# Negated softmax scale folded into the query weights of a decoder layer's attention

## The reference

```python
q = _mxfp4_matmul(x, wq_codes, wq_scales) + bq      # w = codes * repeat(scales, 32, axis=0)
k = _mxfp4_matmul(x, wk_codes, wk_scales) + bk
v = _mxfp4_matmul(x, wv_codes, wv_scales) + bv
...                                                  # 16 heads of 128
scores = jnp.einsum('bqhd,bkhd->bhqk', q, k) / jnp.sqrt(jnp.float32(HEAD_DIM))
attn = jax.nn.softmax(scores, axis=-1)
out = jnp.einsum('bhqk,bkhd->bqhd', attn, v).reshape(B, S, NUM_HEADS * HEAD_DIM)
return _mxfp4_matmul(out, wo_codes, wo_scales) + bo
```

## Time and profile before

| | before |
|---|---|
| median of 3 runs | 530.16 us (528.49 to 530.91) |
| span of the profiled execution | 527.9 us |
| PE busy | 489.7 us, 93% |
| DVE busy | 405.2 us, 77% |
| ACT busy | 283.8 us, 54% |
| POOL busy | 191.0 us, 36% |

### The profile page before, as it was taken

One profiled execution on the slowest core, in us unless ns is written; L12 is line 12 of the kernel. 1 busy time (PEld: TensorE's weight loads), 2 busy tenths in 40 slices (PEclk: granted clock), 3 DMA queues, 4 the chain that ended last, 5 costly groups with the idle time before them and its releaser, 6 DMA issues.

```text
span 527.9 us, 11484 instructions
## 1 busy us (share of the span) xinstructions
PE 489.7 (93%) x3222; PEld 431.4 (82%) x3222; DVE 405.2 (77%) x1040; ACT 283.8 (54%) x804; POOL 191.0 (36%) x232
## 2 busy tenths in 40 slices
PE   6899999999999999999999998979998999898985
PEld 6688899899898898898898898769875667776764
DVE  6689988988988988988988888787784753344465
ACT  2667656655655666666656564655425545522231
POOL 3417512312313313303303034426116666365640
PEclk9999999999999999999999999999989999999999
DMA  6441211210211211211100793299953456445544
GB/s 191 120 116 57 74 32 31 71 30 30 70 30 30 70 30 30 70 30 39 60 0 0 268 324 129 89 296 305 292 186 100 146 175 213 132 128 158 153 145 159
DMA packets 63269, 60.77 MB, mean 115 GB/s; under 512 B 5552, under 2 KB 60544, under 8 KB 63104
## 3 DMA queue, kind: packets, MB, share of 16 engines
q1 hardware_dynamic: 59024, 49.64, 31.0%
q0 software_dynamic: 3936, 10.55, 7.2%
q10 hardware_dynamic: 272, 0.13, 0.1%
HBM read 47.82 MB, written 20.87 MB: 130 GB/s over the span
## 4 chain that ended last, share of the span: by engine, by line
PE 63%; DVE 18%; issue 6%; ACT 6%; POOL 3%; DMA 1%; another core or an unknown queue 1%; DVEq 0%; SPq 0%; ACTq 0%; POOLq 0%
PE bank L998 12%; PE bank L1000 11%; PE bank L999 11%; PE bank L1239 11%; PE bank L1247 6%; DVE qk_lo L1759 4%; DVE rmax L1767 3%; DVE nmax L1771 3%; PE bank L1079 3%; ACT qk_hi L1497 2%; ACT prob L1505 2%; PE bank L1243 2%; DVE pT_lo L1792 1%; PE bank L1004 1%; PE bank L1373 1%
## 5 line engine op out<-in xcount | busy, mean ns | idle before, releaser
L1505 ACT ACTIVATE prob<-bank,nmax 128x256 f32<-128x256 f32 x128 | 59.5, 470 | 105.2 <-DVE nmax L1771 103.3
L711 POOL TENSOR_TENSOR w_lo<-st_c,w_hi 128x512 fp32r<-128x512 f32 x32 | 41.2, 1286 | 197.0 <-ACT w_hi L1468 197.0
L1239 PE MATMUL bank<-moe_w,xT 128*128 x252 | 66.0, 385 | 2.0 <-DVE xT L2067 1.8
L1759 DVE SCALAR_TENSOR_TENSOR qk_lo<-bank,b_col,qk_hi 128x512 fp32r<-128x512 f32 x64 | 47.8, 748 | 14.3 <-ACT qk_hi L1497 13.5
L998 PE MATMUL bank<-hT_hi,w_lo 128*128 128x512 f32 x128 | 52.7, 412 | 4.5 <-DVE qk_lo L1759 3.3
L1767 DVE TENSOR_REDUCE rmax<-bank 128x2 f32<-128x512 f32 x64 | 43.8, 685 | 13.8 <-PE bank L1000 13.3
L1239 PEld LDWEIGHTS bank<-moe_w,xT 128*128 128x128 f32 x252 | 45.2, 190 | 8.7 <-issue 2.9
L1000 PE MATMUL bank<-hT_hi,w_hi 128*128 128x512 f32 x128 | 50.6, 395 | 0.0
L999 PE MATMUL bank<-hT_lo,w_hi 128*128 128x512 f32 x128 | 50.5, 394 | 0.0
L1497 ACT ACTIVATE qk_hi<-bank,b_col 128x512 fp32r<-128x512 f32 x64 | 44.0, 687 | 8.6 <-PE bank L1000 7.2
L1785 DVE TENSOR_SCALAR prob<-prob,rinv 128x256 f32<-128x256 f32 x128 | 46.3, 403 | 2.3
(11 more groups left out here) (272 smaller groups left out, 1493.2 us busy)
## 6 DMA issues: line engine op xcount, KB each, us to landing
y_dram<-ysb SPq DMA_DIRECT2D x63, 128.0 KB
moe_w<-in_w_gate SPq DMA_DIRECT2D x8, 512.0 KB, 8.1
moe_w<-in_w_up SPq DMA_DIRECT2D x8, 512.0 KB, 7.8
moe_w<-in_w_down SPq DMA_DIRECT2D x4, 1024.0 KB, 9.0
st_c<-in_wq_codes SPq DMA_DIRECT2D x16, 128.0 KB
st_c<-in_wk_codes SPq DMA_DIRECT2D x16, 128.0 KB
st_c<-in_wv_codes SPq DMA_DIRECT2D x8, 256.0 KB
st_c<-in_wo_codes SPq DMA_DIRECT2D x8, 256.0 KB
```

Of the source, the lines that this page charges most:

```text
L1239: mm = pe.matmul(o, xT_of(kt), w, start=kt == 0, stop=kt == KT - 1)
L1505: ex = act.activation(prob[:, i % 4, qt, :], bS[i % 2][:, qt * S:(qt + 1) * S], ACT.Exp, bias=nmax[:, i % 2, qt:qt + 1], scale=SCALE, accu ...
L1759: dve.scalar_tensor_tensor(out=qk_lo[:, hp, m, n * HALF:(n + 1) * HALF], in0=src[:, :], scalar=b_col[:, bass.ds(g_h + m * H, 1)], in1=qk_h ...
```

## The change

The query scales are multiplied by `-SCALE` on GpSimd before they meet the codes, and the query bias by `-SCALE` on DVE when the bias columns are copied. So the score block in PSUM is already the negated, scaled score. Its row minimum is the negated row maximum of the scaled scores, which is what the exponential needs as its bias: `exp(-1.0 * block + minimum)`. The multiplication in `maxima` and the tensor `rmax` go, and with them the waits for `v_m1` and `a_exp` there. The reduction's own wait for `t_sc` covers the latter, since TensorE had waited for the same count of `a_exp` before these scores. Apart from that, the one load of four registers in the tail becomes four loads with bounds.

```diff
-        rmax = sb("rmax", [P, 2, 2])
...
-        p_wm = sem("p_wm")
+        p_wm, p_q = sem("p_wm"), sem("p_q")
...
-        v_m1, v_max = sem("v_m1"), sem("v_max")
+        v_max = sem("v_max")
...
+            scaled = [0]
+
+            def scale_queries(c):
+
+                scaled[0] += 1
+                pool.tensor_scalar(st_s[c][:, 0, :], st_s[c][:, 0, :], -SCALE, None, ALU.mult).then_inc(p_q, 1)
+                pool.wait_ge(p_q, scaled[0])
+
             def prep(c, wm, load_count, into):
 
                 wait(pool, d_w[c], load_count)
+                if c in (H0, H1):
+                    scale_queries(c)
...
-            at = [pool.alloc_register(f"need{k}") for k in range(TOPK)]
             pool.wait_ge(v_slot, S_NEED)
             apart(pool)
-            pool.reg_load(at, need[0:1, :])
+            needed = [pool.value_load(need[0:1, k:k + 1], min_val=1, max_val=TILES) for k in range(TOPK)]
...
-                pool.wait_ge(y_done, pool.snap(at[k], min_val=1, max_val=TILES))
+                pool.wait_ge(y_done, needed[k])
...
                     ex = act.activation(prob[:, i % 4, qt, :], bS[i % 2][:, qt * S:(qt + 1) * S], ACT.Exp,
-                                        bias=nmax[:, i % 2, qt:qt + 1], scale=SCALE,
+                                        bias=nmax[:, i % 2, qt:qt + 1], scale=-1.0,
                                         accum_out=rsum[:, i % 2, qt:qt + 1])
...
-            dve.tensor_copy(b_col[:, :], bJ[0][:, 0:3 * H]).then_inc(v_b, 1)
+            dve.tensor_scalar(b_col[:, 0:H], bJ[0][:, 0:H], -SCALE, None, ALU.mult)
+            dve.tensor_copy(b_col[:, H:], bJ[0][:, H:3 * H]).then_inc(v_b, 1)
...
-                dve.tensor_reduce(rmax[:, i % 2, :], bS[i % 2][:, :].rearrange("p (q k) -> p q k", q=2),
-                                  AX.X, ALU.max).then_inc(v_m1, 1)
-                wait(dve, v_m1, p + 1)
-                wait(dve, a_exp, p - 1 if not (pl.first and i < 2) else 0)
-                dve.tensor_scalar(nmax[:, i % 2, :], rmax[:, i % 2, :], -SCALE, None, ALU.mult).then_inc(v_max, 1)
+                dve.tensor_reduce(nmax[:, i % 2, :], bS[i % 2][:, :].rearrange("p (q k) -> p q k", q=2),
+                                  AX.X, ALU.min).then_inc(v_max, 1)
```

## The result

The kernel after runs in 516.36 us (median of 4 runs, 515.0 to 519.73), the kernel before beside it in 529.35 us (4 runs, 528.49 to 530.91). The ratio is 0.974, with a 95% interval of 0.971 to 0.978: 13.0 us less.

The account below looks back on a forecast made before the run. TensorE waiting on stalled VectorE in the attention was taken as the bound. 7.2 + 2.4 + 0.8 - 0.5 = 9.9 us off the profiled 527.9 gives 518.0; with 2.3 for the runs' median, 520.5 us was forecast, range 516.5 to 526.0.

Parts of the forecast that it names:

- The bound and the mechanism: Attention: TensorE waits 1.2 us per group for `qk_lo`, late because DVE's `nmax` multiplication waits out running GpSimd instructions.
- Steady groups: Groups 1 to 6 of the attention: all three late projection tiles recovered, 1.2 us per group, 7.2 us gained.
- slot 7: Steady-group slot: `qk_lo` starts at 169.6 instead of 170.95, so TensorE's second wait goes with 0.9 us to spare.
- slot 0: Steady-group slot: `qk_lo` ends at 175.1, bank wanted at 175.9, so TensorE's third wait goes with 0.8 us to spare.
- First group: First attention group: 0.9 us for the `v_lo` wait, 0.9 for two others, 0.2 for each early pair; 2.4 us gained.
- Last group: Last attention group, with one stalled `nmax` of 0.75 us: 0.8 us gained, bounded by 0 and 1.8.
- three early pairs: First group: pairs whose chain runs through `nmax` to the exponential, each expected to gain 0.2 us.
- The start: Before the first projection: GpSimd's added multiplication delays L708 and L711 under DVE's L948; -0.5 us, between 0 and -1.3.
- The tail: Four register loads instead of one, 3.1 us against 0.777, hidden with 1.5 us to spare: 0.
- Rival 1: DVE's stall moves from `nmax` to the L1785 pair and half of TensorE's waits stay: 525.5 us, chance 0.15.
- Rival 2: Attention ends earlier, but the expert part starts where it did or its own stalls eat it: 529.5 us, chance 0.05.
- Rival 3: Slower: GpSimd's added multiplication keeps L1785 stalled, DVE sets the pace in slots 6 to 0; 535.2 us, chance 0.04.

Follow-up runs that it names:

- reduce_back: Kernel after with the removed 128x2 step put back on VectorE as a one-element tensor_reduce: 502.10 us, ratio 0.981 to the kernel before.
- multiply_back: Kernel after with the 128x2 multiplication put back on VectorE (by 1.0), everything else of the change kept: 507.96 us, ratio 0.992 to the kernel before.
- added_scale_only: Kernel before plus the four bounded loads and one GpSimd multiplication of the query scales by 1.0 before the codes' multiplication: 506.69 us, ratio 0.990.
- loads_only: Kernel before with only the tail's one register load replaced by four bounded loads: 512.11 us, ratio 1.001.
- whole_again: The kernel after, unchanged, run again beside the kernel before on another chip: 499.55 us, ratio 0.976.
- the first and the third set: Experiment sets on different chips, each with the kernel after unchanged beside the kernel before: 499.55 against 511.8 us, and 499.52 against 512.32 us.

## Why the prediction was right or wrong

**The bound and the mechanism: right.** The view that mattered was TensorE's timeline from start to start. Reversing only the stall (`reduce_back` against `multiply_back`) moves the kernel by 5.9 us, which shows that it is the stall and not the work of the small multiplication that the kernel paid for.

**Steady groups: 7.2 forecast, 7.6 measured** (1.27 a group). I had counted 1.04 us of late starts and up to 0.3 of restarts, 1.34 in all, and rounded down to 1.2 without a row for the discount. The period's 38.80 - 37.55 says that nearly all of it came back. The walk through the slots held: slot 7 had 1.0 us to spare (0.9 forecast) and slot 0 had 0.6 (0.8 forecast).

**First group: 2.4 forecast, 2.7 measured. Last group: 0.8 forecast, 0.9 measured.** Both sums were near. Of the first group's parts, the wait of 0.91 at 47.70 and the two like those of the steady groups are gone, as forecast. The 0.2 for each of three early pairs is not borne out: TensorE's three early waits for `qk_lo` were 0.34, 0.48 and 0.47 us and are now 0.23, 0.48 and 0.47. What else makes up the 2.7 stays open. In the last group one wait of 0.88 us for `pT_lo` at 318.09 is gone, and those of 0.70 and about 0.5 stay.

**The start: the term that was mis-sized and had the wrong sign, -0.5 forecast, +0.6 measured.** The step that failed was that L708, moved later by 0.64 us, would only fall deeper under the L948 multiplications, so that their rows would come out at 11.3 instead of 10.8 "and the transposes, and all that follows, wait for them". It overlooked that L708 already held up a smaller operation in front of them, L938, for 1.13 us. What the shift does depends on when the scales land. At 6.94, within 0.03 of the landing that the forecast was worked out from, it all but ends that stall, and the rows are done 0.85 us earlier (`added_scale_only`); with 6.76 they are done at 9.80 (`reduce_back`). At 6.49 and 6.71 the stall stays, and the rows come at 10.99 and 11.21 against 10.93 in `loads_only`: 0.1 to 0.3 later. In the profiled execution of the kernel after, the scales landed at 7.58, after the small operations were through. So the sign of the term was wrong at the very landing it was worked out from, as far as one execution tells, and part of the 0.6 measured is the luck of a late landing. This term alone is 1.1 us, over half of the 1.95 by which the attention beat the forecast.

**The tail: 0 forecast, 0 measured**, as `loads_only` shows, and the first gather still waited for TensorE:

```profile
449.26 1.14 POOL L907 DMA_INDIRECT yg<-y_dram,y_slot  x1 [1.69 <-PE bank L1247]
```

**The sum.** The attention gave 11.85 us instead of 9.9: 1.1 of the difference is the start, 0.3 the first group, 0.4 the steady ones, 0.1 the last. The kernel before had a median of 529.35 instead of 530.16 in the comparison, which is another 0.8. The other 1.1 or so of the 13.0 lies behind the attention, where the forecast had everything shift as a block; 1.1 us of the 12.3 in `whole_again` are left for it too, so that scatter may not be all of it, and its cause stays open. The whole gain of the kernel after in the first and the third set was 12.3 and 12.8 us. The range ended too high by 0.14 us: its lower edge of 516.5 was the full recovery of every term, 516.9, and 0.4 us more, which left nearly nothing for the scatter of the measurement. Without the start's 1.1 us, for one, the time would lie inside.

**Rival 1, the stall moves: its mechanism is there and its price is not.** It gave 0.94 us per pair in three slots; the pairs took 1.39 and 2.06 us at 159.75 and 164.47, and 11.3 us more over the kernel. The price rested on half of TensorE's waits staying, and none of the three of a steady group stayed, for the reason that the prediction gave against it: the awaited tile stands ahead of the pair.

**Rival 2** didn't come: the expert part started earlier by what the attention gained. **Rival 3**, with GpSimd's added instruction as a cost, was wrong in its sign in a way that none of my cases held. In the kernel before the same instruction is a gain of 4.9 us, because it moves the long instructions to where they stall something harmless. That doesn't appear in the change's total, since the removal takes the same stalls away.

## What to carry to other kernels

Where an operation of one engine waits out whole instructions of another, as the 128x2 multiplication did here, the cost of a small operation is set by what it meets and by who stands behind it: look for durations far above the median of the same group, then for the engine that waits for the instruction behind. A tiny step between a producer and a consumer on the critical side is worth removing, or giving to an operation that is not stalled (here the reduction, in none of 64 cases), even if the stall then moves to a larger instruction, as long as what is waited for is issued ahead of that one. Before crediting an added or removed instruction with a gain, put the same work where it moves nothing: here that separated 4.9 us of timing from 0 us of work.

## What the runs showed of the hardware that I had not expected

An added GpSimd instruction of 0.56 us made a kernel 4.9 us faster, and two of them made it 1.7 us slower (ratios 0.990 and 1.003).

TensorE's 40 warm matmuls at the start, from 4.03 us on, took between 6.1 and 7.6 us in executions of kernels that are alike there. The windows of `reduce_back` and `multiply_back` show the rate change at different times (PE busy and its matmuls in brackets come first, clock third from the end):

```profile
7.00:8.00 1.00, 1.00 (x6) 1.00 (x6) 0.90 (x4) 0.00 (x0) 0.92 (x2) 1.00 0.99 327
...
9.00:10.00 1.00, 1.00 (x7) 1.00 (x7) 1.00 (x4) 0.33 (x1) 0.52 (x1) 1.00 0.72 219
10.00:11.00 1.00, 1.00 (x10) 1.00 (x10) 1.00 (x4) 0.00 (x0) 0.94 (x1) 1.00 0.73 177
```

```profile
6.00:7.00 1.00, 1.00 (x7) 1.00 (x7) 0.66 (x7) 0.21 (x1) 0.00 (x0) 1.00 0.73 175
7.00:8.00 1.00, 1.00 (x10) 1.00 (x10) 0.86 (x5) 0.00 (x0) 0.46 (x1) 1.00 1.00 336
```

Six or seven matmuls of 128x128 start in each microsecond until about 10 us in the one and until about 7 in the other, and ten or eleven after it, while the granted clock reads 1.00 (full speed, 2.4 GHz) throughout. What makes the rate rise, and when, these rows don't tell.

The same kernels took 17 us less in the sets of experiments than in the first pair, all of it behind the attention (195.5 us in the profile of the kernel before, 177.6 in that of `loads_only`), with the attention equal within 0.2 us. That is more than the whole gain of the change, so kernels can only be compared beside each other on one chip.
